# Graph network and expert feed-forward in one kernel: the feed-forward products go from fp32 to split 16-bit, with a software pipeline over groups of three tiles

## Chip, cores and metric

The kernel runs on one core of one Trainium2 chip. The metric is the device time of one execution in microseconds (us), as the median of several runs. The traces below come from one profiled execution.

## What is computed

`x` has 6250 rows of 256 features. A four-layer graph network is added to it; then a feed-forward part with two experts out of eight, chosen once for all rows, is added. Cut to what matters here:

```python
# graph part: 100,000 edges, 4 layers
h = layernorm(x) @ W_in + b_in
for l in range(4):
    msg = segment_sum((h * dinv)[src], dst) * dinv
    z = relu((h + msg) @ Wl[l] + bl[l] + mean(h) @ Wg[l] + bg[l])
    h = layernorm(z) * gamma[l] + beta[l]
x = x + h
# feed-forward part: the routing sees the mean over all rows, so both experts serve every row
xf = layernorm(x)
top_i, top_w = top2(softmax(scaled softmax(mean(xf) @ Wr + br)))
for e in top_i:                       # W1[e]: 256 x 512, W2[e]: 512 x 256
    h = gelu(xf @ W1[e] + b1[e]);  y += top_w[e] * (h @ W2[e] + b2[e])
x = x + layernorm(y + xf) * fgamma + fbeta
```

## The kernel before

The rows are cut into 49 tiles of 128 rows (`T`; the last, `LAST`, has 106). The kernel is written by hand, engine by engine: each engine has a program of its own, and semaphores (`wait_ge`) order them. No scheduler moves anything. Four stages follow each other.

First the adjacency counts are built and written to memory (to 548 us in the trace). Then come four graph layers, to 2806 us: for each of 49 tiles TensorE adds 49 products of 128x512 (`aggregate`, L1416), and inside this row of products it does the transposes and the six 16-bit products of the tile before (`turn_u` L1364 before product 14, `product_u` L1374 before product 24). VectorE has a chain of some fourteen instructions for each tile beside that (L923 to L840). GpSimd (Pool) does nothing there but, in the last layer, fetch `x` again (L604). Then the routing picks the two experts (`topi`), and SyncE loads their weights (L548, L553).

The feed-forward stage works on groups of three tiles (`SUP = RING = 3`, `LOOP = 16` groups and one more for tile 48). For a group TensorE does `up`: eight blocks `f` of hidden units, for each `KC = 2` products of 128 columns of `W1_s` with 384 rows of `xfT` in fp32. ScalarE applies Gelu from PSUM to SBUF (L1221, tile `gT`). Then come `turn` for the next group's three tiles (L1479, each copied from PSUM by ScalarE, L1216), and `down`: three tiles, each `TOP * FC = 8` fp32 products of 256 columns (L1496). An fp32 product is two MATMUL instructions in the trace. VectorE then normalizes each tile (`result`: L1027 adds the bias, L1031 and L1033 take mean and variance, Pool computes the inverse root, L610 and L612, and L1035 to L1044 finish). The loop over groups is a loop of the engines' programs, not written out.

The upward products wait for PSUM banks 0 to 2 in turn: block `f` waits for the Gelu of block `f - 3`. The downward products wait for all eight Gelus of their own group.

## Time and profile before

| | |
|---|---|
| median of 3 runs | 3208.35 us (3207.71 to 3212.56) |
| profiled execution, its own time | 3210.56 us |
| its span from the first to the last instruction | 3208.6 us |
| TensorE busy | 3076.7 us, 96% of the span |
| VectorE busy | 1901.3 us, 59% |
| ScalarE busy | 855.9 us, 27% |
| GpSimd (Pool) busy | 70.3 us, 2% |
| mean granted TensorE clock | 0.975 of full speed |
| by the chain that ended last | TensorE 84%, ScalarE 9%, VectorE 3% |

A row of the page or of a view gives line, engine, operation, the output and input tiles, shapes and a count; then busy time and the mean duration of one. A line number is a line of the kernel before. "PEld" is TensorE loading weights, which overlaps its products.

### The profile page before, as it was taken

The page shows a single profiled execution, that of the slowest core. Times are in us where ns is not written, and L with a number is a line of the kernel's source. Part 1 is how long each engine was busy: PE and PEld are TensorE (multiplying, and loading weights), DVE is VectorE, ACT ScalarE, POOL GpSimd, SP SyncE. Part 2 cuts the span into 40 slices and gives each one's busy share as a digit, 9 for nine tenths or more (in the row PEclk, how much of TensorE's full clock was granted, in tenths as well). Part 3 has the DMA queues.
Part 4 walks back from the last instruction along what each step waited for, and adds up shares of the span by engine and source line. Part 5 has one row for each costly group of instructions (what it writes and reads, how often), then busy time and mean ns, then how long its engine had stood idle before and what let it go on. Part 6 is the DMA issues. An engine that isn't in the chain of part 4 may idle for free.

```text
span 3208.6 us, 54202 instructions
## 1 busy us (share of the span) xinstructions
PE 3076.7 (96%) x17323; PEld 1804.0 (56%) x17323; DVE 1901.3 (59%) x5185; ACT 855.9 (27%) x1934; POOL 70.3 (2%) x168
## 2 busy tenths in 40 slices
PE   6999996999999999999999999999999999979998
PEld 4777773444444444444444444444444444468887
DVE  8999997555555545555554555555566666645554
ACT  4989896111111111111111111111111111132332
POOL 0000000000000000000000000000000000001010
PEclk9989996999999999999999999999999999989999
DMA  4323324122222222222222222222222222110000
GB/s 130 96 83 94 91 82 122 61 70 70 70 70 70 70 70 70 70 70 70 70 70 70 70 70 70 70 70 70 80 82 82 82 82 82 48 40 16 18 18 18
DMA packets 134110, 225.11 MB, mean 70 GB/s; under 512 B 12277, under 2 KB 106596, under 8 KB 134018
## 3 DMA queue, kind: packets, MB, share of 16 engines
q1 hardware_dynamic: 131666, 217.53, 20.9%
q0 software_dynamic: 2352, 6.40, 0.8%
q8 instruction: 52, 0.85, 0.1%
q14 instruction: 40, 0.33, 0.0%
HBM read 178.17 MB, written 45.74 MB: 70 GB/s over the span
## 4 chain that ended last, share of the span: by engine, by line
PE 84%; ACT 9%; DVE 3%; issue 2%; DMA 1%; SPq 0%; DVEq 0%; ACTq 0%; POOLq 0%; POOL 0%
PE bank L1416 64%; ACT tab L1094 7%; PE bank L1490 5%; PE bank L1496 5%; PE bank L1374 4%; PE bank L1364 1%; PE bank L1266 1%; PE bank L1286 1%; DVE later L757 1%; DMA tab<-in_x 1%; DVE region L724 1%; PE bank L1310 1%; ACT later L1118 0%; PE bank L1304 0%; ACT xnb L1112 0%
## 5 line engine op out<-in xcount | busy, mean ns | idle before, releaser
L1416 PE MATMUL bank<-tab,region 128*128 128x512 f16 x9604 | 2143.2, 380 | 14.3 <-DVE tab L840 14.0
L1416 PEld LDWEIGHTS bank<-tab,region 128*128 128x128 fp8e4 x9604 | 940.8, 98 | 1065.5 <-DVE tab L840 17.9
L1094 ACT ACTIVATE tab<-later 128x539 fp8e4<-128x539 uint8 x588 | 336.1, 674 | 1.9 <-DVE later L757 1.9
L724 DVE TENSOR_SCALAR region<-iota_w,src_col,src_w 128x540 bf16<-128x540 int16 x858 | 310.8, 415 | 0.4 <-issue 0.3
L941 DVE SCALAR_TENSOR_TENSOR region<-bank,c_back,later 128x256 f32<-128x256 f32 x196 | 94.8, 484 | 351.2 <-PE bank L1374 351.2
L1197 ACT ACTIVATE sd<-mv,eps_c 128x1 f32<-128x1 f32 x196 | 57.8, 295 | 817.6 <-DVE mv L948 817.6
L936 DVE TENSOR_TENSOR region<-bank,region 128x256 f16<-128x256 f32 x196 | 83.3, 425 | 287.7 <-ACT region L1193 287.7
L1193 ACT ACTIVATE region<-bank 128x256 f16<-128x256 f32 x196 | 75.3, 384 | 568.2 <-PE bank L1364 568.2
L1490 PE MATMUL bank<-tab 128*128 128x384 f32 (+1 forms) x544 | 178.0, 487 | 3.8 <-DMA b_s<-in_L_ffn_b 3.8
L1496 PE MATMUL bank<-tab 128*128 128x256 f32 (+1 forms) x784 | 175.5, 384 | 0.9 <-ACT tab L1221 0.9
L1490 PEld LDWEIGHTS bank<-tab 128*128 128x128 f32 x544 | 164.4, 310 | 13.4 <-issue 6.3
L1374 PE MATMUL bank<-later,region 128*128 128x256 f16 x1176 | 161.0, 273 | 0.9 <-DVE region L936 0.9
L1496 PEld LDWEIGHTS bank<-tab 128*128 128x128 f32 (+1 forms) x784 | 148.8, 192 | 22.3 <-ACT tab L1221 1.4
L1191 ACT ACTIVATE region<-bank 128x256 f32<-128x256 f32 x196 | 75.3, 384 | 294.0 <-PE bank L1416 294.0
L1161 ACT ACTIVATE tab<-region,c_write 128x256 f32 x147 | 74.6, 508 | 274.1 <-DVE region L957 274.1
L1374 PEld LDWEIGHTS bank<-later,region 128*128 128x128 f16 x1176 | 115.2, 98 | 56.3 <-DVE region L936 1.2
L1221 ACT ACTIVATE tab<-bank,b_s 128x384 f32<-128x384 f32 (+1 forms) x136 | 77.2, 568 | 249.3 <-PE bank L1490 249.3
L1286 PE MATMUL bank<-region 128*128 128x270 bf16 x900 | 131.0, 299 | 1.3 <-DVE region L708 0.8
L1286 PE MATMUL bank<-region,later 128*128 x864 | 129.3, 309 | 1.4 <-DVE region L724 1.4
L925 DVE TENSOR_TENSOR region<-bank,region 128x256 f32<-128x256 f32 x196 | 83.0, 423 | 73.9 <-ACT region L1191 73.9
L1286 PEld LDWEIGHTS bank<-region,later 128*128 128x128 f16 x864 | 112.7, 145 | 15.4 <-issue 2.5
L1286 PEld LDWEIGHTS bank<-region 128*128 128x128 f16 x900 | 108.7, 146 | 19.9 <-DVE region L724 1.8
(199 smaller groups left out, 2232.8 us busy)
## 6 DMA issues: line engine op xcount, KB each, us to landing
region<-adjacency SPq DMA_DIRECT2D x196, 784.0 KB, 4.3
adjacency<-tab SPq DMA_DIRECT2D x12, 3136.0 KB, 13.7
region<-in_x POOLq DMA_DIRECT2D x48, 128.0 KB, 2.3
out<-region SPq DMA_DIRECT2D x48, 128.0 KB, 1.7
tab<-in_x SPq DMA_DIRECT2D x1, 6016.0 KB
tab<-in_L_ffn_W SPq DMA_DIRECT2D x4, 512.0 KB, 4.7
region<-in_L_gnn_Wl SPq DMA_DIRECT2D x1, 1024.0 KB, 5.4
later<-in_L_gnn_Wg SPq DMA_DIRECT2D x1, 1024.0 KB, 9.4
```

The lines of the kernel that those rows point to most:

```text
L724: v.tensor_scalar(hot_s[:, j, :], iota_w[:, 0:WP], src_col[:, ds(first_block[0] + j, 1)], src_w[:, ds(first_block[0] + j, 1)], ALU.is_equa ...
L925: tile_own.done(v.tensor_tensor(acc_s, acc[a][:, 0:D], lo_f[:, a, :], ALU.add))
L936: v.tensor_tensor(uT[:, 1, :, :], T3[3], uT[:, 0, :, :], ALU.subtract).then_inc(uT_split, 1)
L941: tile_own.done(v.scalar_tensor_tensor(out=Z, in0=bank[4][:, 0:D], scalar=c_back[:, ds(n, 1)], in1=bias[:], op0=ALU.mult, op1=ALU.add))
L1094: ins = a.activation(stage[h][:, :, slot, f * LANES:f * LANES + n], counts[:, :, 0:n], ACT.Copy, saturate=False)
L1191: a.activation(lo_f[:, s, :], acc[s][:, D:2 * D], ACT.Copy).then_inc(lo_ready, 1)
L1221: a.activation(gT[:, f, 0:w], bank[f % 3][:, 0:w], ACT.Gelu, bias=b1_s[:, f // FC, f % FC:f % FC + 1]).then_inc(gelu_done, 1)
L1286: ins = mm(bank[k % 2 * 2 + half][:, 0:HALFP], hot_d[m % 2][:, :, j], hot_s[:, block + j, half * HALFP:(half + 1) * HALFP], start=j == 0, ...
L1374: ins = mm(bank[4][:, 0:D], uT[:, a, k, :], Wx[:, b, l, k, :], start=q == 0, stop=q == len(parts) - 1)
L1416: ins = mm(acc[a][:, :], A_s[:, a, m, :], tab[:, here + m, :], start=m == 0, stop=m == T - 1)
L1490: ins = mm(bank[f % 3][:, 0:w], W1_s[:, f // FC * KC + k, f % FC:FF:FC], xfT[:, k, 0:w], start=k == 0, stop=k == KC - 1)
L1496: ins = mm(bank[5 + u][0:r, 0:D], gT[:, f, u * P:u * P + r], W2_s[:, f // FC, f % FC, :], start=f == 0, stop=f == TOP * FC - 1)
```

## The change

The feed-forward products take 16-bit operands. Each fp32 operand is scaled and split into a high part (`fp16(scale * a)`) and a low part (what is left of it, also fp16), and three of the four products are added: high x high, high x low, low x high (`SPLIT`).

The weights are split once after they are loaded (ScalarE `w1_high_part`, `w2_high_part`; VectorE `w1_low`, `w2_low`). The transposed rows are split for each tile (ScalarE `xf_high`, VectorE `xf_low`), and the Gelu's output for each block (ScalarE `gelu`, two ACTIVATEs now, and VectorE `g_low`). The scales need bounds on the weights of all eight experts. They are made on Pool beside the first graph layer: it fetches `W1`, `W2` and `b1` of all experts in 32 pieces of 128x512 and one small one, squares each and adds it up. One 24-column product, one square root and some small VectorE instructions turn the sums into scales.

```diff
+            def fetch(c):
+                if c > 1:
+                    pool.wait_ge(scan_done, c - 1)
...
+                    nc.gpsimd.dma_start(scan_s[c % 2].rearrange("p (e c) -> p e c", e=EX),
+                                        pieces[c]).then_inc(scan_in[c % 2], 16)
...
+            for c in range(len(pieces)):
+                fetch(c + 1)
+                m = sums[c // each]
+                hold(pool, scan_in[c % 2], (c // 2 + 1) * 16)
+                square(scan_s[c % 2])
+                if c:
+                    pool.wait_ge(scan_done, c)
+                nc.gpsimd.tensor_tensor(m, m, scan_s[c % 2].rearrange("p (e c) -> p e c", e=EX),
+                                        ALU.add).then_inc(scan_done, 1)
```

The bias and the residual are added ahead of time on Pool, two additions of 128x256 for each tile; VectorE's part of a tile is five instructions instead of nine:

```diff
+            def residuals(t):
+                r = rows(t)
+                if t >= 3 * SUP:
+                    pool.wait_ge(y_taken, t - 3 * SUP + 1)
+                hold(pool, xf_ready, t + 1)
+                nc.gpsimd.tensor_tensor(xfb[0:r, t % (3 * SUP), :], xf_s[0:r, t % (2 * SUP), :], b2c[0:r, :],
+                                        ALU.add).then_inc(pre_done, 1)
+                nc.gpsimd.tensor_tensor(H[0:r, t, :], H[0:r, t, :], fbet[0:r, :], ALU.add).then_inc(pre_done, 1)
```

`gx`, the split Gelu output, has two buffers, and the loop is written out. TensorE now does all upward products of group `i`, then the transposes of group `i + 1`, then the downward products of group `i - 1`:

```diff
-                pe.wait_ge(gelu_done, (i + 1) * F8)
...
-                    pe.wait_ge(out_ready, (i + 1) * SUP)
-                    down(i * F8, u, P)
...
+            for i in range(GR + 1):
+                if i < GR:
+                    for f in range(TOP * FC):
+                        up(i, f)
+                for u in range(in_group(i + 1)):
+                    turn((i + 1) * SUP + u)
+                for u in range(in_group(i - 1)):
+                    down((i - 1) * SUP + u)
```

ScalarE's work for one block:

```diff
+            def gelu(i, f):
...
+                act.wait_ge(up_done, q + 1)
+                if q >= RING:
+                    act.wait_ge(g_split, q - RING + 1)
+                a.activation(gT[:, q % RING, 0:w], bank[q % RING][:, 0:w], ACT.Gelu, bias=b1_s[:, e, f % FC:f % FC + 1],
+                             scale=e_sel[:, e, 2:3]).then_inc(gelu_done, 1)
...
+                act.wait_ge(gelu_done, q + 1)
+                a.activation(gx[:, i % 2, 0, f, 0:w], gT[:, q % RING, 0:w], ACT.Copy,
+                             scale=g_scale[:, e:e + 1]).then_inc(g_high, 1)
```

TensorE, from the last upward block of a group to the next group, in the loop before (bank 3 and 4 hold transposes, banks 5 to 7 a tile's result):

```order
L1490 MATMUL bank1<-tab 128x384 [waits gelu_done]
L1490 MATMUL bank1<-tab 128x384
...
L1479 MATMUL bank3<-ident,region 128x128 [waits xf_ready]
...
L1479 MATMUL bank4<-ident,region 128x128 [waits xf_ready]
...
L1479 MATMUL bank3<-ident,region 128x128 [waits xfT_copied,xf_ready]
...
L1496 MATMUL bank5<-tab 128x256 [waits out_ready,ew_ready,gelu_done]
L1496 MATMUL bank5<-tab 128x256 x7
L1496 MATMUL bank6<-tab 128x256 [waits out_ready]
```

And the same place now, in the second turn of the loop:

```order
L1708 MATMUL bank0<-tab 128x384 [waits gelu_done]
L1708 MATMUL bank0<-tab 128x384 x5
L1693 MATMUL bank3<-ident,tab 128x128 [waits xfT_split,xf_ready]
...
L1693 MATMUL bank4<-ident,tab 128x128 [waits xfT_split,xf_ready]
...
L1693 MATMUL bank3<-ident,tab 128x128 [waits xfT_split,xf_ready]
L1693 MATMUL bank3<-ident,tab 128x128
L1723 MATMUL bank5<-tab,region 128x256 [waits w2_split,g_split]
L1723 MATMUL bank5<-tab,region 128x256 x23
L1723 MATMUL bank6<-tab,region 128x256 [waits w2_split,g_split]
```

A block is six 16-bit products for two fp32 ones, and a tile's downward row 24 for eight. The third transpose, which uses bank 3 again, waited for ScalarE's copy of the first; now it waits for VectorE's low part of the first (`xfT_split`).

VectorE, one turn of the loop now (L1191 is `g_low`, L1147 `xf_low`, L1142 `xf`, L1199 to L1215 the end of a tile of the group before):

```order
L1191 SCALAR_TENSOR_TENSOR region<-region,g_scale 128x384 [waits g_high] x8
L1147 SCALAR_TENSOR_TENSOR tab<-bank3,tab 128x2x128 [waits xfT_copied]
L1142 TENSOR_SCALAR tab<-tab,mv_all,rstd_all 128x256 [waits pre_done,xfT_done]
L1147 SCALAR_TENSOR_TENSOR tab<-bank4,tab 128x2x128 [waits xfT_copied]
...
L1199 SCALAR_TENSOR_TENSOR region<-bank5,y_scale,layer_rows 128x256 [waits pre_done,down_done]
L1202 BN_STATS st<-region 128x6 [waits y_taken]
L1204 BN_AGGR mv<-st 128x2 [waits dve_route]
L1209 SCALAR_TENSOR_TENSOR region<-region,mv,fgam 128x256 [waits fvar_ready]
L1215 SCALAR_TENSOR_TENSOR region<-region,rs,tab 128x256 [waits pre_done,out_out0,frstd_ready,dve_route]
```

Before, one tile's part was this, and nothing of the Gelus stood in VectorE's row:

```order
L1024 TENSOR_SCALAR region<-tab,mv_all,rstd_all 128x256
L1027 TENSOR_TENSOR region<-bank,tab 128x256 [waits down_done]
...
L1029 TENSOR_TENSOR region<-region 128x256 [waits dve_ffn]
...
L1031 BN_STATS st<-region 128x6 [waits dve_ffn]
...
L1033 BN_AGGR mv<-st 128x2 [waits dve_ffn]
L1035 TENSOR_SCALAR region<-region,mv,rs 128x256 [waits frstd_ready]
...
L1037 TENSOR_TENSOR region<-region,fgam 128x256 [waits dve_ffn]
...
L1039 TENSOR_TENSOR region<-region,fbet 128x256 [waits dve_ffn]
```

So the eight low parts and the first `xf_low` stand ahead of the tiles of the group before, and the third transpose, with all downward products behind it on TensorE, waits for them.

## Rows read from the trace of the kernel before

**Rows 1.** Window of the feed-forward loop: PE, PEld, DVE, ACT, POOL busy; PE clock.

```profile
2828.40:3185.60 357.20, 347.82 (x1373) 312.46 (x1374) 181.18 (x469) 107.88 (x189) 34.15 (x92) 0.99 0.06 19
```

**Rows 2.** Timeline of one group: start, us, engine, line (last: the next group).

```profile
3008.47 10.50 PE L1490 MATMUL bank<-tab 128*128 128x384 f32 x32
...
3009.98 0.58 ACT L1221 ACTIVATE tab<-bank,b_s 128x384 f32<-128x384 f32 x1 [10.03 <-PE bank L1490]
...
3020.25 10.59 PE L1496 MATMUL bank<-tab 128*128 128x256 f32 x48
...
3030.68 9.53 PE L1490 MATMUL bank<-tab 128*128 128x384 f32 x29
```

**Rows 3.** Timeline of the last layer: 16-bit products by their start times.

```profile
2782.72 2.32 PE L1416 MATMUL bank<-tab,region 128*128 128x512 f16 x10
...
2784.88 0.82 PE L1374 MATMUL bank<-later,region 128*128 128x256 f16 x6
...
2785.53 8.58 PE L1416 MATMUL bank<-tab,region 128*128 128x512 f16 x39
```

**Rows 4.** Groups by line, feed-forward stage: Gelu; busy, mean ns of one, idle.

```profile
L1221 ACT ACTIVATE tab<-bank,b_s 128x384 f32<-128x384 f32 x128 | 74.4, 582 | 233.9 <-PE bank L1490 233.9
...
L1221 ACT ACTIVATE tab<-bank,b_s 128x106 f32<-128x106 f32 x8 | 2.8, 350 | 15.5 <-PE bank L1490 15.5
```

**Rows 5.** Groups by line, first 548 us: ScalarE with two per-partition operands.

```profile
L1112 ACT ACTIVATE xnb<-tab,xnb_bias,xrs 128x256 f32<-128x256 f32 x49 | 28.9, 590 | 3.4 <-DVE xnb_bias L747 3.4
```

**Rows 6.** The page's costliest groups.

```profile
L941 DVE SCALAR_TENSOR_TENSOR region<-bank,c_back,later 128x256 f32<-128x256 f32 x196 | 94.8, 484 | 351.2 <-PE bank L1374 351.2
...
L1161 ACT ACTIVATE tab<-region,c_write 128x256 f32 x147 | 74.6, 508 | 274.1 <-DVE region L957 274.1
...
L1286 PEld LDWEIGHTS bank<-region,later 128*128 128x128 f16 x864 | 112.7, 145 | 15.4 <-issue 2.5
```

**Rows 7.** Timeline: VectorE behind a tile's downward products.

```profile
3001.77 0.42 DVE L1027 TENSOR_TENSOR region<-bank,tab 128x256 f32<-128x256 f32 x1 [4.59 <-PE bank L1496]
...
3004.56 0.41 DVE L1035 TENSOR_SCALAR region<-region,mv,rs 128x256 f32<-128x256 f32 x1 [1.09 <-POOL rs L612]
```

**Rows 8.** Windows, columns as in Rows 1: the granted clock around gaps.

```profile
290.30:293.70 3.40, 2.41 (x56) 2.02 (x56) 3.40 (x12) 3.06 (x9) 0.00 (x0) 1.00 0.02 5
293.80:297.10 3.30, 3.30 (x17) 2.46 (x16) 3.30 (x13) 2.69 (x6) 0.00 (x0) 0.50 0.00 0
...
2802.00:2806.00 4.00, 1.02 (x6) 0.29 (x5) 2.38 (x7) 1.06 (x3) 0.00 (x0) 0.99 0.00 0
2806.00:2828.00 22.00, 5.05 (x22) 3.22 (x22) 10.45 (x42) 4.37 (x13) 0.00 (x0) 0.50 0.23 65
...
2840.00:2843.50 3.50, 2.90 (x15) 2.34 (x14) 0.00 (x0) 2.28 (x6) 0.00 (x0) 1.00 0.00 0
```

**Rows 9.** Timeline: the first group's upward products.

```profile
2828.43 12.97 PE L1490 MATMUL bank<-tab 128*128 128x384 f32 x32 [3.79 <-DMA b_s<-in_L_ffn_b]
```

**Rows 10.** Timeline of a first-layer tile: VectorE's chain and TensorE.

```profile
700.73 0.49 DVE L929 SCALAR_TENSOR_TENSOR region<-region,c_own 128x256 f32<-128x256 f32 x1
...
702.09 0.38 PE L1364 MATMUL bank<-ident,region 128*128 128x128 f32 x2
...
710.04 0.49 DVE L840 SCALAR_TENSOR_TENSOR tab<-region,c_write,tab 128x256 f32 x1 [0.49 <-ACT tab L1161]
...
711.14 0.42 DVE L925 TENSOR_TENSOR region<-bank,region 128x256 f32<-128x256 f32 x1
```

**Rows 11.** Groups by line: Pool.

```profile
L595 POOL IOTA rep<- 128x2304 f16 x1 | 4.3, 4276 | 0.0
...
L573 POOL MEMSET tab<- 128x256 f32 x1 | 0.3, 312 | 0.2 <-POOL tab L569 0.2
```

**Rows 12.** Timeline: the last, 106-row group, and the last VectorE instruction.

```profile
3185.53 7.59 PE L1490 MATMUL bank<-tab 128*128 128x106 f32 x32
...
3203.86 0.42 DVE L1044 TENSOR_TENSOR region<-region,tab 106x256 f32<-106x256 f32 x1
```

More of the change, by code:

```diff
@@ L73 @@
 SUP = RING
+GR = LOOP + 1
+ZSCALE = 1024.0
+TINY = 1e-15
+SCAN = 512
 TURN_AT, PRODUCT_AT = 0, 8
@@ new lines, in square, with total @@
+            def square(x):
+                own.done(nc.gpsimd.tensor_tensor(x, x, x, ALU.mult))
+                own.hold()
+            def total(sums, width, to):
+                while width > 1:
+                    width //= 2
+                    own.hold()
+                    own.done(nc.gpsimd.tensor_tensor(to if width == 1 else sums[:, :, 0:width], sums[:, :, 0:width],
+                                                     sums[:, :, width:2 * width], ALU.add))
+            sums = [w[:, 0:SCAN].rearrange("p (e c) -> p e c", e=EX) for w in (src_col, src_w)]
@@ new lines, in _ @@
+            for m in sums:
+                own.done(nc.gpsimd.memset(m, 0.0))
+            own.wait()
+            fetch(0)
+            for c in range(len(pieces)):
[7 more added lines that the diff above has]
+                                        ALU.add).then_inc(scan_done, 1)
@@ L601, in again @@
+            hold(pool, scan_done, len(pieces))
+            hold(pool, scan_in[0], (len(pieces) // 2 + 1) * 16)
+            for k, m in enumerate(sums):
+                total(m, width, e_lim[:, k * EX:(k + 1) * EX].unsqueeze(2))
+            square(scan_s[0][:, 0:EX * FC])
+            total(scan_s[0][:, 0:EX * FC].rearrange("p (e c) -> p e c", c=FC), FC, e_lim[:, 2 * EX:].unsqueeze(2))
+            own.wait()
+            pool.sem_inc(lim_set, 1)
             def again(t, i, u, r):
@@ L1058, in _ @@
-            route_own.wait()
-            dve.sem_inc(ew_ready, 1)
-            with dve.Fori(0, LOOP - 1) as i:
+                xf(SUP + u)
+            w1_low(1)
+            dve.wait_ge(b2_in, 16 * TOP)
+            own.done(v.tensor_scalar(b2c[:], b2_s[:, 0, :], topw[:, 0:1], None, ALU.mult))
+            own.wait()
+            v.scalar_tensor_tensor(out=b2c[:], in0=b2_s[:, 1, :], scalar=topw[:, 1:2], in1=b2c[:],
+                                   op0=ALU.mult, op1=ALU.add).then_inc(ew_ready, 1)
@@ new lines, in ffn, with mine, before, after @@
+            def ffn(i):
+                def mine(f):
+                    if i < GR:
+                        g_low(i, f)
+                def before(u, step):
+                    if u < in_group(i - 1):
+                        step((i - 1) * SUP + u)
+                def after(u):
+                    if u < in_group(i + 1):
+                        xf_low((i + 1) * SUP + u)
+                    if u < in_group(i + 2):
+                        xf((i + 2) * SUP + u)
+                for f in range(TOP * FC):
+                    mine(f)
@@ L1073, in _ @@
+                    before(u, result)
+                if i == 0:
+                    for a in range(TOP):
+                        w2_low(a)
+            for i in range(GR + 1):
+                ffn(i)
         @block.scalar
@@ L1457, in _ @@
                 general()
+            pe.wait_ge(lim_set, 1)
+            mm(bank[6][:, 0:3 * EX], ones[:], e_lim[:], start=True, stop=True).then_inc(lim_sum, 1)
             pe.wait_ge(hsum_ready, LAYERS + 1)
```

314 lines of the change are left out of this document (214 added, 100 removed).

## The prediction, made before the changed kernel ran

> **What bounds the kernel now.** I read the busy times by stage first. The change touches two places: the feed-forward stage from 2828.43 us on, and Pool in the first layer. In the feed-forward loop TensorE is busy 347.8 of 357.2 us [rows 1], so it is the bound there, and the chain of waits says the same. The timeline of one group shows how: 32 upward instructions in about 10.5 us, transposes, 48 downward ones in about 10.6, and the next group 22.2 us after the last (3030.68 - 3008.47) [rows 2]. ScalarE has one Gelu of 0.58 us for every 1.29 us of upward work and waits for TensorE in between; it is far from a bound. Two readings of the same trace then decide what replaces this: what the new ScalarE and VectorE work costs, and what TensorE's clock does after a gap.
>
> **TensorE's work.** 16-bit products stream at a pace that depends on their columns: ten of 512 columns start in 2.16 us (2784.88 - 2782.72), 0.216 each; six of 256 in 0.65 us (2785.53 - 2784.88), 0.108 each [rows 3]. A product of 384 columns is halfway, 0.162. An upward block of six is 0.97 us, a group's eight blocks 7.8 us. Three tiles of 24 downward products are 72 x 0.108 = 7.8 us. The weights of the upward products are read with a step of four elements. A strided 16-bit weight load took 145 ns with a step of 18 elements [rows 6], still under 162, so I cost it at nothing; if it passed 162 it would add 48 times the excess to a group. Alone TensorE would need about 16 us for a group against 22.2, and the loop would win some 95 us. It will not be alone.
>
> **ScalarE's work.** For each block it now has a Gelu with two per-partition operands and a copy from SBUF with one. Two operands took 590 ns and one 508 for 256 columns [rows 5, 6], so the second costs 0.08 and the Gelu becomes 0.582 + 0.08 = 0.66. The slope is (582 - 350) / (384 - 106) = 0.83 ns a column [rows 4], so the copy, 508 ns at 256, becomes 0.61 at 384. The copy waits for the Gelu's own end (I take 0.04 for the hand-over), and the next Gelu may start about 0.1 before the copy ends. That is 1.22 us for a block. It is longer than the 0.97 that TensorE takes, but TensorE may be three blocks ahead, so its upward row still ends after 7.8 us; ScalarE ends after 0.97 + 0.22 (from a block's last product to its Gelu: 3009.98 - 3008.47 - 1.29 [rows 2]) + 8 x 1.22 + 0.1 = 11.1 us.
>
> **Where the stall goes.** The order of the instructions puts the third transpose behind `xfT_split` of the first tile. ScalarE's copies of the transposes stand behind its eighth block, and VectorE's `xf_low` behind its eighth `g_low`. A VectorE instruction of this kind took 484 ns at 256 columns [rows 6]; at 384 I take 0.62 (between 0.48 and 0.73, one and a half times it). So: 11.1 + 0.65 (`g_low`) + 0.5 (`xf_low`) + 0.3 (third transpose and the first weights) = 12.5, and 12.5 + 7.8 = 20.3 us for a group, at full clock. TensorE does nothing but four small transposes between 7.8 and 12.2 us. This stall is in each of the 16 full groups but for the last, which has a small group behind it. What comes late next are the downward products.
>
> **The clock.** A gap like this is in the trace. Between 2802 and 2806 us TensorE was busy 1.0 of 4.0 us, and the granted clock is 0.50 (1.2 GHz) afterwards; in 290.3 to 293.7, with 2.4 us of busy time that was mostly 49 one-column products, it fell too, and the next 3.3 us have 0.50. In the loop of before, 2840 to 2843.5, TensorE was busy 2.9 of 3.5 us and the clock stayed at 1.00 (2.4 GHz) [rows 8]. The new gap, some 0.7 us of work in 4.5, looks like the two that fell. What a low clock costs: the first group's 32 upward instructions, begun at it, took 12.97 us where the same row took 10.50 [rows 2, 9], 2.5 us. If the low stretch is as short as the one in rows 8 (3.3 us) and lies wholly over downward products, it costs half of that, 1.65. I take 1.8 (bounds 0 and 2.5), and the group becomes 22.1 us, almost what it was.
> The Trainium skill (TensorE: Matmul & The Clock Gate, section HAM oscillation) says the same of loops: a wait in every turn that puts the engine idle for several microseconds brings the half clock back in every turn, and its cost is paid each time. It speaks against this change; without that rule the group would be 20.3.
>
> **VectorE behind the products.** From L1027 to the end of Pool's answer took 2.79 us (3004.56 - 3001.77) [rows 7]. One addition goes (0.46), the fused one is 0.06 longer, and one of 0.48 follows: 2.9 us for a tile, while its products take 2.6. So VectorE ends a group 12.5 + 2.6 + 3 x 2.9 = 23.8 us after its start, 3.5 us into the next at full clock, and then does `g_low` of block 0 (to 4.1). ScalarE needs that for its fourth Gelu, at 1.2 + 3 x 1.22 = 4.9. The cover is 0.8 us; a tile of over 3.2 us uses it up.
>
> **The loop's sum.** The first group has no downward row: at the low clock its first block takes 1.95, so 1.95 + 0.22 + 9.9 + 0.65 + 0.5 + 0.3 = 13.5. Fifteen groups at 22.1 are 331.5. Then come the 106-row group (48 products bound by weight loads of about 0.1 us, 4.8), 7.8 and 2.6 of downward products, a wait for VectorE's tiles (about 3), a last tile of 2.9, and about 1 of low clock: 22. Together 367.0 us. Before, from 2828.43 to the end of the last VectorE instruction (3204.28) it was 375.9 [rows 9, 12]. The loop gives 9 us.
>
> **Setup.** The weight loads are issued at the same point. Behind their landing stand now two splits of an expert's first half on ScalarE (0.7 each) and VectorE (0.75); but the first expert's matrix no longer waits for the second's. Bounds -0.5 and +2; I take +0.3. The new root and scale instructions lie beside the routing sum, which waits for TensorE anyway.
>
> **Pool in the first layer.** 32 pieces, each a fetch, a square and an addition of 128x512, and four rows of halving sums. The trace has no such instruction. The nearest are a memset of 256 columns in 0.31 us and an iota at 1.86 ns a column (4276 / 2304) [rows 11]; so 0.6 to 1.9 us each, and I take 1.0, 64 us of work spread over 150 to 200 us of transfers. Nobody waits for it. It costs only if it slows VectorE, of which the trace shows nothing: no arithmetic of Pool on 128 columns or more runs beside VectorE's there. In this layer VectorE has little to spare. U is ready at 701.22 and TensorE's transpose starts at 702.09, 0.9 us; the chain's end at 710.53 is 0.6 before the next tile's L925 at 711.14 [rows 10]. Bounds: 0, and 30 us if each of 64 instructions holds VectorE for half its length and no slack takes it. Against some 15 tiles with 0.9 us of slack each, I take 6 us.
>
> **Sum.** 3210.56 (this execution's own time; the median is 2.2 lower) - 9 + 0.3 + 6 = 3207.9; against the median, 3205.7. I write 3206: no change that a measurement of this kernel can tell, which is about 0.2%, 6.4 us. Its own range is 3194 to 3216.
>
> **Rivals.**
> *The clock holds.* The two new gaps in rows 8 that fell had less work than 0.7 us in 4.5, or one-column work; the new one has four transposes, and if ScalarE's pair is 1.15 instead of 1.22 the gap is 0.6 shorter. Then 13.5 + 15 x 20.3 + 21 = 339 us, 37 less than before: 3208.35 - 37 + 6.3 = 3178. Chance 0.17.
> *Pool's scan holds VectorE.* Place: the first layer, from 548 us. Pool's squares and additions and VectorE's instructions take turns at the memory; each holds the other up. VectorE's chain has at most 0.9 us to give to a tile, so it decides once the delays pass that: nine of its instructions read two tensors or one at double pace, and three delays of 0.5 us in a tile are 1.5, 0.6 over. At half of 1.0 us for 64 instructions, 30 us: 3208.35 - 9 + 30 = 3229. For it: VectorE's small slack. Against it: transfers of 256-byte pieces leave Pool waiting most of the time. Chance 0.2.
> The Trainium skill (SBUF — State Buffer, section Who interferes with whom) states such a lock between a GpSimd instruction that reads and a VectorE instruction with two SBUF inputs; no run here shows it yet.
> *VectorE's tiles become the bound.* Pool now has two additions a tile (0.5 to 1.0 us each by rows 11) beside its 0.75 us for the root. If they delay VectorE's last instruction so that a tile takes 3.9 us instead of 2.9, `g_low` of block 0 ends at 7.1 instead of 4.1, 2.2 past ScalarE's need: a group of 23.5 or so with some low clock, 15 x 1.4 more: 3227. It decides from 3.2 us on. Chance 0.12.
> *The split is cheaper than I think* (a copy of 0.5, say): 8 x 0.11 less a group, 14 us: 3192. Chance 0.06.
> The forecast keeps 0.45.
>
> **How the numbers follow.** The forecast lies around 3206 with about half of it between 3202 and 3215, a third of it below. Faster by over 0.2% (under 3202): 0.17 + 0.06 + 0.45 x 0.35 = 0.39. Slower (over 3215): 0.2 x 0.75 + 0.12 + 0.45 x 0.1 = 0.31. Same: 0.30. The range leaves out a piece of the first two rivals at either side: 3176 to 3230.
>
> **What would show it.** Right: upward rows of 48 in 7.8 us; a gap of about 4 us ahead of each third transpose, released by VectorE's L1147; windows of 0.50 clock in the downward rows; groups 22 us apart; ScalarE pairs of 1.22; in the first layer steps of 11.5 to 12.5 us while Pool scans. Wrong: groups at 20 us with the clock at 1.00 throughout; layer steps of 13 us; a first-layer stage more than 15 us longer; L1191 of block 0 as the releaser of the fourth Gelu. An upward row that stretches beyond 7.8 us (strided weights) would make it wrong too.

## The result and the profile after

The changed kernel takes 3261.3 us (median of 4, 3256.0 to 3265.6) against 3208.0 (3207.5 to 3212.6): the ratio is 1.0165, interval 1.0153 to 1.0177. It is 53 us slower, and 31 us above the upper end of my range.

By stages (the windows of the kernel after; each row has the stretch, its length, the busy time of PE, its weight loads, DVE, ACT and POOL, then the granted clock):

```profile
548.00:1106.00 558.00, 522.09 (x2537) 253.88 (x2538) 305.63 (x686) 72.05 (x183) 112.35 (x115) 0.97 0.25 81
1106.00:2806.00 1700.00, 1698.30 (x8448) 835.07 (x8447) 910.41 (x2444) 218.11 (x593) 24.18 (x45) 1.00 0.22 73
...
2860.00:3200.00 340.00, 262.50 (x1746) 192.99 (x1746) 210.51 (x417) 159.80 (x285) 115.21 (x174) 0.92 0.07 22
```

Two stages have holes in TensorE's time. In the first layer (548 to 1106) it is idle for 36 of 558 us, and Pool, which had almost nothing to do there, is busy for 112. In the feed-forward loop it is idle for 77 of 340 us, and the clock is 0.92 in the mean. The loss is counted from the starts of TensorE's rows. The first tile's product in the first layer began at 567.08 before and begins at 573.02 now; the last tile's began at 2805.96 and now begins at 2842.06:

```profile
573.02 0.82 PE L1583 MATMUL bank<-later,region 128*128 128x256 f16 x6
590.59 0.82 PE L1583 MATMUL bank<-later,region 128*128 128x256 f16 x6
```
```profile
2842.06 0.98 PE L1583 MATMUL bank<-later,region 128*128 128x256 f16 x6 [0.94 <-DVE region L1045]
2864.61 10.55 PE L1708 MATMUL bank<-tab 128*128 128x384 f16 x48 [3.63 <-DVE tab L1180]
2880.80 9.32 PE L1708 MATMUL bank<-tab 128*128 128x384 f16 x48 [1.17 <-DVE tab L1147]
```

So the layers are 36.1 us longer: 5.9 ahead of the first product, and 30 in the next six steps, which take 17.6, 14.9, 15.6, 19.6, 14.3 and 16.6 us where each took 11.45 (578.53 less 567.08, say). The seventh takes 11.65, and behind it the steps are as before. From there to the first upward product it is 22.6 us, as before (22.5 to the row of [rows 9]). The loop, to the end of VectorE's last instruction, takes 391.1 us instead of 375.9 [rows 9, 12]: 15.2 more. Together that is 51.4, the difference of the two spans.

**The first layer.** VectorE's groups of instructions from 575 to 640 us, while Pool scans the weights (busy us, mean ns, then the idle time before them):

```profile
L1063 DVE TENSOR_TENSOR region<-region,layer_rows 128x256 f32<-128x256 f32 x4 | 6.9, 1719 | 0.3 <-DVE region L1061 0.2
L954 DVE SCALAR_TENSOR_TENSOR later<-region,valid,later 128x256 f32<-128x256 f32 x4 | 6.1, 1524 | 0.4
L1061 DVE TENSOR_SCALAR region<-region,mv,rs 128x256 f32<-128x256 f32 x4 | 3.6, 910 | 0.1
L1055 DVE BATCH_NORM_STATS2 st<-region 128x6 f32<-128x256 f32 x4 | 1.7, 428 | 0.4
L1045 DVE TENSOR_TENSOR region<-bank,region 128x256 f16<-128x256 f32 x4 | 1.7, 425 | 4.4 <-ACT region L1375 4.4
```
and Pool's in the whole scan (the 16 squares of the other buffer, the row of `dstf`, waited 3.1 us for their transfers):
```profile
L660 POOL TENSOR_TENSOR srcf<-srcf 128x512 f32<-128x512 f32 x16 | 16.8, 1049 | 2.9 <-DMA srcf<-in_L_ffn_W 2.6
L653 POOL DMA_DIRECT2D dstf<-in_L_ffn_W x16 | 15.0, 936 | 4.8 <-POOL src_col L681 2.1 <-POOL src_w L681 2.1 <-POOL src_w L671 0.3
L681 POOL TENSOR_TENSOR src_col<-src_col,dstf 128x512 f32<-128x512 f32 x8 | 10.4, 1301 | 1.1
```

The multiplication by gamma (L1063) reads two tensors of SBUF: 1719 ns. L1061 reads one: 910, and it took 412 without the scan (s0_no_scan below). The two that stay at their length, 425 and 428 ns, read one operand from PSUM (L1045), or take statistics of one tensor (L1055). Pool's own instructions hardly wait for VectorE: all 32 squares take 1.03 to 1.05 us and 30 of the 32 additions 1.26 to 1.27; only two take 1.53. And Pool waited for data for only 2.6 and 3.1 us in front of its 32 squares.

**The loop.** One group on the timeline (start, duration, and in brackets the wait and its releaser):

```profile
3037.01 0.53 PE L1693 MATMUL bank<-ident,tab 128*128 128x128 f32 x2 [3.98 <-DVE tab L1147]
3037.33 9.62 PE L1723 MATMUL bank<-tab,region 128*128 128x256 f16 x72
3041.74 0.48 DVE L1199 SCALAR_TENSOR_TENSOR region<-bank,y_scale,layer_rows 128x256 f32<-128x256 f32 x1 [3.01 <-PE bank L1723]
3043.20 0.41 POOL L702 TENSOR_SCALAR sd<-mv 128x1 f32<-128x1 f32 x1 [14.29 <-DVE mv L1204]
3043.76 0.55 POOL L704 TENSOR_TENSOR rs<-sd,half_c 128x1 f32<-128x1 f32 x1
3044.28 0.73 POOL L711 TENSOR_TENSOR layer_rows<-tab 128x256 f32<-128x256 f32 x1
3044.40 0.89 DVE L1215 SCALAR_TENSOR_TENSOR region<-region,rs,tab 128x256 f32<-128x256 f32 x1 [0.83 <-POOL rs L704]
3044.96 0.91 POOL L713 TENSOR_TENSOR tab<-tab,fbet 128x256 f32<-128x256 f32 x1
3045.21 0.47 DVE L1199 SCALAR_TENSOR_TENSOR region<-bank,y_scale,layer_rows 128x256 f32<-128x256 f32 x1
3046.78 6.01 PE L1708 MATMUL bank<-tab 128*128 128x384 f16 x36
3052.11 2.13 DVE L1191 SCALAR_TENSOR_TENSOR region<-region,g_scale 128x384 f16<-128x384 f32 x3
3053.29 0.67 ACT L1421 ACTIVATE region<-bank,b_s,e_sel 128x384 f32<-128x384 f32 x1 [1.39 <-DVE region L1191]
3054.01 2.44 PE L1708 MATMUL bank<-tab 128*128 128x384 f16 x12 [1.22 <-ACT region L1421]
3060.87 0.50 PE L1693 MATMUL bank<-ident,tab 128*128 128x128 f32 x2 [3.98 <-DVE tab L1147]
```
and two windows, the start of its downward row and the whole group behind it (columns as before; the granted clock is the number behind POOL's):
```profile
3037.30:3040.60 3.30, 3.30 (x18) 2.35 (x16) 1.28 (x4) 0.38 (x1) 0.00 (x0) 0.50 0.00 0
3046.80:3070.60 23.80, 18.50 (x128) 13.73 (x126) 14.37 (x30) 10.55 (x19) 7.49 (x13) 0.93 0.06 17
```

The gap ahead of the third transpose is where I put it, 3.98 us. The 72 downward products behind it take 9.62 us, the first 3.3 of them at a clock of 0.50. VectorE's three tiles start 3.45 us apart (3041.74, 3045.21, 3048.66); its last instruction of a tile, L1215, takes 0.89 us beside Pool's L711 and L713. So the first `g_low` comes at 3052.11, and it takes 1.08 us itself, beside the third tile's L713 on Pool, where it is 0.61 in the kernel without the additions. The fourth Gelu waits 1.39 for it, and TensorE, at most three blocks ahead, waits 1.22. The group takes 23.86 us; it was 22.2 [rows 2].

### The profile page after: what moved, and what is told of

It reads as the page before. It is cut to its first block, busy times and chain, and to the rows that moved or that the text cites. A ratio compares the mean times of both kernels' runs of the same rounds, so it can differ in the third digit from the quotient of the medians.

```text
span 3260.0 us, 55441 instructions
## 1 busy us (share of the span) xinstructions
PE 3025.1 (93%) x17989; PEld 1705.5 (52%) x17989; DVE 1994.0 (61%) x5193; ACT 924.9 (28%) x2064; POOL 271.9 (8%) x380
## 4 chain that ended last, share of the span: by engine, by line
PE 73%; ACT 11%; DVE 7%; issue 5%; POOL 1%; DMA 1%; DVEq 1%; SPq 0%; ACTq 0%; POOLq 0%
PE bank L1625 61%; ACT tab L1276 7%; PE bank L1583 4%; PE bank L1723 2%; ACT region L1421 2%; PE bank L1573 1%; PE bank L1475 1%; PE bank L1495 1%; POOL rs L704 1%; DVE later L866 1%; DMA tab<-in_x 1%; DVE region L1199 1%; DVE st L1202 1%; POOL sd L702 1%; PE bank L1519 1%
## 5 line engine op out<-in xcount | busy, mean ns | idle before, releaser
L1625 PEld LDWEIGHTS bank<-tab,region 128*128 128x128 fp8e4 x9604 | 942.3, 98 | 1069.7 <-DVE tab L949 17.6
L1045 DVE TENSOR_TENSOR region<-bank,region 128x256 f16<-128x256 f32 x196 | 83.3, 425 | 281.7 <-ACT region L1375 281.7
L695 POOL DMA_DIRECT2D region<-in_x x49 | 26.4, 540 | 2107.6 <-DVE tab L1075 2106.2
L1708 PE MATMUL bank<-tab 128*128 128x384 f16 (+1 forms) x816 | 140.5, 327 | 26.0 <-ACT region L1421 19.7
L1723 PE MATMUL bank<-tab,region 128*128 128x256 f16 (+1 forms) x1176 | 154.5, 301 | 0.0
L1723 PEld LDWEIGHTS bank<-tab,region 128*128 128x128 f16 (+1 forms) x1176 | 127.9, 109 | 24.6
L1421 ACT ACTIVATE region<-bank,b_s,e_sel 128x384 f32<-128x384 f32 (+1 forms) x136 | 87.7, 645 | 168.3 <-PE bank L1708 147.4
L1708 PEld LDWEIGHTS bank<-tab 128*128 128x128 f16 x816 | 88.3, 115 | 74.4 <-ACT region L1421 32.2
```

The lines of the kernel that those rows point to most:

```text
L1045: v.tensor_tensor(uT[:, 1, :, :], T3[3], uT[:, 0, :, :], ALU.subtract).then_inc(uT_split, 1)
L1421: a.activation(gT[:, q % RING, 0:w], bank[q % RING][:, 0:w], ACT.Gelu, bias=b1_s[:, e, f % FC:f % FC + 1], scale=e_sel[:, e, 2:3]).then_in ...
L1625: ins = mm(acc[a][:, :], A_s[:, a, m, :], tab[:, here + m, :], start=m == 0, stop=m == T - 1)
L1708: ins = mm(bank[q % RING][:, 0:w], W1x[:, b, f // FC * KC + k, f % FC:FF:FC], xfT[:, i % 2, c, k, 0:w], start=n == 0, stop=n == 3 * KC - 1)
L1723: ins = mm(bank[5 + u][0:r, 0:D], gx[:, i % 2, b, f, u * P:u * P + r], W2x[:, c, f // FC, f % FC, :], start=n == 0, stop=n == 3 * TOP * FC ...
```

## The experiments

Two losses, each with a candidate: Pool's scan in the first layer, and Pool's additions in the loop. Behind them stands the third question, whether the gap and the clock cost what I said. The names that begin with s concern the scan, those with g the loop, those with c both.

**s0_no_scan**: the scan is replaced by constants.

```diff
-            for c in range(len(pieces)):
-                fetch(c + 1)
...
-                square(scan_s[c % 2])
...
+            own.done(nc.gpsimd.memset(e_lim[:, 0:EX], 4.0))
```

> The whole scan is left out: the bounds of the weights are three constants, so scales and output differ. In the trace of the changed kernel the first layer's products begin 5.9 us later than before and their first seven steps take 30.1 us more than 11.45 each. Theory A (the scan costs all of that): first product back at 567 us, all steps 11.45, layers 36 us shorter, 3261 - 36 = 3225. Theory B (the start of the layers is later for another reason, as the moved rows of layer weights or the longer program): the steps come back but not the 5.9 before them: 3231. Rival: the loss was in neither, and the time stays above 3250.

3227.5 us (3224.9 to 3228.9), ratio to before 1.0062 [1.0045, 1.0079]: 33.8 less than the changed kernel. The first product begins at 564.7 and all steps are 11.45:

```profile
564.68 0.82 PE L1567 MATMUL bank<-later,region 128*128 128x256 f16 x6
```

L1063's counterpart is back at its length (VectorE's groups of this kernel, 575 to 640 us):

```profile
L938 DVE SCALAR_TENSOR_TENSOR later<-region,valid,later 128x256 f32<-128x256 f32 x6 | 2.9, 484 | 0.8
L1047 DVE TENSOR_TENSOR region<-region,layer_rows 128x256 f32<-128x256 f32 x6 | 2.6, 426 | 0.2
L1045 DVE TENSOR_SCALAR region<-region,mv,rs 128x256 f32<-128x256 f32 x6 | 2.5, 412 | 0.2
```

The whole loss of the layers, the 5.9 us at their start among it, is the scan's: without its arithmetic the first product begins at 563.4 to 566.5 us in the traces (six kernels), with the whole of it at 570.5 to 573.4 (five). That start moves by some 3 us from trace to trace.

**s1_fetch_only** and **s2_arith_only**: its two halves.

```diff
 s1_fetch_only
                 hold(pool, scan_in[c % 2], (c // 2 + 1) * 16)
-                square(scan_s[c % 2])
...
+                pool.sem_inc(scan_done, 1)
 s2_arith_only
-                fetch(c + 1)
-                hold(pool, scan_in[c % 2], (c // 2 + 1) * 16)
                 square(scan_s[c % 2])
```

> The 32 transfers stay, with their waits; squares, additions and sums on Pool are left out, the bounds are constants (output differs). Theory A (Pool's arithmetic holds VectorE): within 3 us of the kernel without any scan, about 3226, VectorE's additions of two tensors back at 0.42 us. Theory T (the transfers, of 256-byte pieces, or their issue on Pool of 0.92 us each, hold VectorE or the adjacency's transfers): still 20 us or more above it, 3245 to 3260.

> The reverse: 32 squares and 32 additions of 128x512 on Pool back to back on zeros, no transfers, constants as bounds (output differs). Without fetches of 0.92 us in between the 64 instructions take 64 x 1.15 = 74 us instead of 123. Theory A: the loss is one for each Pool instruction that overlaps VectorE's, so it is about as large as before, 25 to 40 us, but in fewer tiles, 4 or 5 instead of 7; 3250 to 3262. Theory T: no loss, 3226.

3227.3 and 3253.4 us (one run each). The 32 transfers with their issue on Pool cost the kernel nothing that shows, though they stretch some of VectorE's instructions a little (one with one SBUF operand, L1051, is 452 ns instead of 412). The arithmetic alone brings 26 of the 34 us back, in three steps of 17.7, 17.3 and 17.3 us and a first product 10 us later. The 8 us that neither half shows by itself come only with both, where the same arithmetic is spread over 126 us instead of 75; what makes them was not tested. Rows of s2_arith_only (VectorE's from 592 to 627 us, then Pool's):

```profile
L1063 DVE TENSOR_TENSOR region<-region,layer_rows 128x256 f32<-128x256 f32 x2 | 2.7, 1372 | 0.1
```
```profile
L660 POOL TENSOR_TENSOR srcf<-srcf 128x512 f32<-128x512 f32 x16 | 18.0, 1126 | 0.0
```

**s5_one_input**: the same transfers, but each Pool instruction reads one operand.

```diff
-                square(scan_s[c % 2])
+                own.done(nc.gpsimd.tensor_scalar(scan_s[c % 2], scan_s[c % 2], 1.0, None, ALU.mult))
...
-                nc.gpsimd.tensor_tensor(m, m, scan_s[c % 2]..., ALU.add).then_inc(scan_done, 1)
+                nc.gpsimd.tensor_scalar(scan_s[c % 2], scan_s[c % 2], 1.0, None, ALU.mult).then_inc(scan_done, 1)
```

> The scan's transfers and waits as in the changed kernel, but each of its 64 Pool instructions of two operands is one of a single operand on the same 128x512 (a product with 1.0); the sums are left out and the bounds are constants. Theory A1 (it is Pool's two reads that hold VectorE): first layer within 5 us of the kernel without a scan: 3228 to 3232. Theory A2 (any Pool instruction that reads SBUF does, by its length): the loss falls only with the length of the instructions, from 1.05 to 1.27 us to perhaps 0.8: 20 to 25 us stay, 3247 to 3252.

3232.6 us (one run): 5 above the kernel without a scan, 29 below the changed one, although Pool's instructions became longer, not shorter (Pool in the scan, then VectorE from 575 to 640 us):

```profile
L678 POOL TENSOR_SCALAR srcf<-srcf 128x512 f32<-128x512 f32 x16 | 24.1, 1507 | 1.0 <-DMA srcf<-in_L_ffn_W 0.5
```
```profile
L1062 DVE TENSOR_TENSOR region<-region,layer_rows 128x256 f32<-128x256 f32 x5 | 3.6, 723 | 0.2
L953 DVE SCALAR_TENSOR_TENSOR later<-region,valid,later 128x256 f32<-128x256 f32 x5 | 2.6, 530 | 0.6
L1060 DVE TENSOR_SCALAR region<-region,mv,rs 128x256 f32<-128x256 f32 x5 | 2.7, 548 | 0.2
```

Theory A2 falls: 97 us of Pool's one-operand work cost 5 us, 75 of its two-operand work (32 squares, 32 additions) cost 34. VectorE's instructions in the rows are still stretched, by 0.05 to 0.3 us instead of 0.5 to 1.3, and most of that goes into the slack of a tile. The edit changes the number of operands and with it the kind of instruction, and no run parts the two.

**g0_no_adds**: the two additions out of the loop.

```diff
-                nc.gpsimd.tensor_tensor(xfb[...], xf_s[...], b2c[0:r, :], ALU.add).then_inc(pre_done, 1)
-                nc.gpsimd.tensor_tensor(H[0:r, t, :], H[0:r, t, :], fbet[0:r, :], ALU.add).then_inc(pre_done, 1)
+                pool.sem_inc(pre_done, 1)
+                pool.sem_inc(pre_done, 1)
```

> Only the feed-forward loop changes: Pool's two additions a tile (expert bias into the normalised rows, beta into the residual) are left out, so the output lacks both and the first reads stale rows. Scan as in the changed kernel. Theory A (they lengthen VectorE's tile from 3.05 to 3.45 us, which delays g_low of the first block and with it the fourth Gelu by 1.39 us): tile 3.05, the fourth Gelu's wait 0.2, its block's stall on TensorE gone, groups 22.6 instead of 23.86, 16 x 1.26 = 20 us less: 3241. Rival: the tile is set by Pool's own root pair (0.41 + 0.55) and stays at 3.4: 3258. Rival: the wait goes but TensorE's gap grows by the same, since ScalarE's eight pairs set it: groups 23.6, 3257.

3240.9 us (3238.1 to 3247.2), ratio 1.0106 [1.0089, 1.0123]: 20.4 less. L1215's counterpart takes its 485 ns again (VectorE's groups of this kernel), tiles are 3.06 us apart, and groups 22.02 and 22.36 in turn behind the first two, 22.2 on the mean; `g_low` of block 0 is back at 0.61 us:

```profile
L1214 DVE SCALAR_TENSOR_TENSOR region<-region,rs,tab 128x256 f32<-128x256 f32 x21 | 10.2, 485 | 17.6 <-POOL rs L704 17.6
```

**g3_filled**: more work in the gap (`FILL` is 30), with the output unchanged.

```diff
+                    if u == 2 and i:
+                        pe.wait_ge(y_taken, (i - 1) * SUP)
+                        for n in range(FILL):
+                            mm(bank[5][:, 0:D], gx[:, i % 2, 0, 0, 0:P], W2x[:, 0, 0, 0, :], ...)
                     turn((i + 1) * SUP + u)
```

> More work and nothing else: in the gap ahead of the third transpose TensorE does 30 products of 256 columns into a bank that is overwritten behind them (3.25 us); the output is unchanged. Theory A (the gap lowers the clock, which costs the downward row 1.7 us a group): clock 1.00 in the loop, 72 downward products in 7.8 instead of 9.6 us; VectorE's tiles then begin 0.9 earlier and the next upward row 1.7 earlier, so the fourth Gelu waits some 0.3 longer; groups 22.4 to 22.6, 15 x 1.3 = 20 us less: 3241. Rival (the downward row is slow from weights or reads, not the clock): groups 23.9, 3261. Rival (the filling delays the transpose): over 3261.

3237.9 us (3236.1 to 3240.5), ratio 1.0092 [1.0075, 1.0109]: 420 more products made the kernel 23.5 us faster. TensorE's rows of this kernel, and one group's window:

```profile
3066.73 3.44 PE L1739 MATMUL bank<-tab,region 128*128 128x256 f16 x30
3070.88 0.41 PE L1694 MATMUL bank<-ident,tab 128*128 128x128 f32 x2 [0.71 <-DVE tab L1148]
3071.13 8.02 PE L1724 MATMUL bank<-tab,region 128*128 128x256 f16 x72
```
```profile
3056.80:3079.00 22.20, 20.16 (x159) 15.88 (x157) 14.41 (x30) 10.55 (x19) 7.56 (x13) 1.00 0.06 20
```

The transpose comes at the same distance from its group's start, released by the same instruction; only the clock differs, 1.00 instead of 0.93, and the downward row takes 8.02 instead of 9.62 us. The group, 22.20 us, is 1.66 shorter: that is the price of the clock, 1.8 in my sum.

**g1_turn_late**: the gap's other cure, by order.

```diff
-                for u in range(in_group(i + 1)):
+                for u in range(min(2, in_group(i + 1))):
                     turn((i + 1) * SUP + u)
-                for u in range(in_group(i - 1)):
+                for u in range(min(2, in_group(i - 1))):
                     down((i - 1) * SUP + u)
+                if in_group(i + 1) > 2:
+                    turn((i + 1) * SUP + 2)
+                if in_group(i - 1) > 2:
+                    down((i - 1) * SUP + 2)
```

> Full computation; only TensorE's order changes: of each group's three transposes the third goes behind two of the three downward tiles, so the 4 us in which TensorE waited for xf_low of the first tile hold 48 downward products. VectorE's order stays: xf_low of the third tile, which now comes late, stands ahead of all three tiles' normalisation. Theory A (a group is upward row, gap and downward row in line, with the clock's fall on top): no gap over 2 us, clock 1.00 in the loop, and VectorE in line becomes the bound: its three tiles (10.4 us) can begin only at about 15 us and end at 25.4, ScalarE's fourth Gelu waits for them, then five more pairs: groups 21 to 22, about 23.86 - 2.2, 15 x 2.2 = 33 us less: 3228, 3220 to 3240. Rival (the gap only moves, to the third transpose's copy): 23 to 24, 3250 to 3262.

3260.0 us (3258.2 to 3261.1), ratio 1.016 [1.0143, 1.0177]: nothing gained, groups 23.9 us. My 3228 was wrong. The downward row is whole, but the gap stands in the upward row now (ScalarE's and TensorE's rows of this kernel, and one group's window):

```profile
3051.40 2.13 DVE L1191 SCALAR_TENSOR_TENSOR region<-region,g_scale 128x384 f16<-128x384 f32 x3
3052.57 0.67 ACT L1421 ACTIVATE region<-bank,b_s,e_sel 128x384 f32<-128x384 f32 x1 [5.08 <-DVE region L1191]
3053.30 4.03 PE L1708 MATMUL bank<-tab 128*128 128x384 f16 x12 [4.91 <-ACT region L1421]
```
```profile
3042.30:3066.20 23.90, 18.99 (x129) 13.98 (x127) 14.32 (x30) 10.55 (x19) 7.57 (x12) 0.86 0.05 17
```

That VectorE's order becomes the bound I had said, at 21 to 22 us; that the new gap lowers the clock again, for longer (0.86 in the group), I had not put into the sum. Behind it twelve products take 4.03 us at a clock of 0.50; at the pace of 36 in 6.01 us (the changed kernel at 3046.78) it would be 2.0.

**g2_tiles_between**: VectorE's order too.

```diff
+                before(i - 2, 1, gathered)
+                before(i - 2, 1, centred)
+                normal_of(1)
+                before(i - 2, 1, result)
...
-                for f in range(TOP * FC):
+                for f in range(1, TOP * FC):
                     mine(f)
...
+                before(i - 1, 0, gathered)
```

> Full computation; TensorE's order as in g1_turn_late, and VectorE's normalisation of the second and third tile of a group stands between the first g_low of the next group, the wait for Pool's root of each tile filled with other work. Theory A (the loss in the loop is order, not work): TensorE has 7.8 + 0.9 + 7.8 = 16.5 us of work for a group at full clock, VectorE about 16, and the groups come 16.5 to 18 us apart with the clock at 1.00; 15 x 6.6 = 99 us less: 3162 (3150 to 3185). Rival (Pool's and VectorE's instructions stretch each other, so VectorE's 16 become 18.5 or more): 19 us, 3190. Rival (ScalarE's chain through the copies of the transposes is the bound): over 20 us, 3205 or more.

3180.0 us (3176.4 to 3182.7), ratio 0.9914 [0.9897, 0.993]: 81 less than the changed kernel, with all of its work, and faster than the kernel before. The gain expected was 99, with groups of 16.5 to 18 us; they are 18.13. VectorE's instructions are still stretched here (L1218, the last of a tile, 906 ns). The clock is 1.00 through the group and the holes are 1.4 of 18.1 us (one group's window of this kernel):

```profile
3039.00:3057.10 18.10, 16.67 (x128) 12.99 (x127) 14.33 (x30) 10.66 (x19) 7.62 (x13) 1.00 0.07 24
```

**s4_scan_on_act**: the scan's arithmetic on ScalarE, in the last layer.

```diff
+                    if last and s < 2:
+                        act.wait_ge(scan_in[s], 16 * (i + 1))
+                        a.activation(scan_s[s], scan_s[s], ACT.Square,
+                                     accum_out=part_sq[:, s, ds(i, 1)]).then_inc(scan_done, 1)
```

> Full computation; the squares and sums of the expert weights go from Pool in the first layer to ScalarE in the last: one piece of 128x512 (2 KB in a row per partition) in two of three tiles, one Square with a running sum each, about 0.7 us, put where ScalarE waits over 4 us for VectorE. Pool keeps only the fetches and the 32 columns of the bias. Theory A (only Pool's arithmetic beside VectorE's costs): first layer as without a scan, last layer 0 to 3 us longer: 3227 to 3230. Rival (ScalarE's extra instruction delays the copies on the tile's chain): 0.7 in 32 tiles, 3250. Rival (the function's table is loaded anew each time, 1.28 us twice per tile): 3290 or more.

3227.3 us (3226.1 to 3228.8), ratio 1.006 [1.0043, 1.0077]: as without a scan. Its 32 squares lie in ScalarE's waits (ScalarE's groups of this kernel, 2260 to 2800 us):

```profile
L1361 ACT ACTIVATE dstf<-dstf 128x512 f32<-128x512 f32 x16 | 9.9, 622 | 0.0
```

**c1_both**, **c2_order**, **c3_early**: all of it together, then two steps more. The edit of c2 to VectorE's order, and that of c3 to Pool's:

```diff
 c2_order
                 before(i - 2, 1, result)
+                mine(0)
                 before(i - 2, 2, gathered)
                 before(i - 2, 2, centred)
                 normal_of(2)
-                mine(0)
+                mine(1)
                 before(i - 2, 2, result)
-                for f in range(1, TOP * FC):
+                for f in range(2, TOP * FC):
 c3_early
             for i in range(GR + 1):
+                for u in range(in_group(i)):
+                    beta(i * SUP + u)
                 for u in range(SUP):
...
-                nc.gpsimd.tensor_tensor(H[0:r, t, :], H[0:r, t, :], fbet[0:r, :], ALU.add).then_inc(pre_done, 1)
```

> Full computation: g2_tiles_between and s4_scan_on_act together. If the two losses are independent the gains add: the one was 3261.3 - 3180.0 = 81.3 us below the changed kernel, the other 34.0: 3146 (3143 to 3150), about 2% faster than the kernel before. Rival (they share something, as the clock or the start of the feed-forward): over 3155.

> c1_both with VectorE's first two g_low of a group one place earlier: the first ahead of the third tile's normalisation, the second ahead of its last instruction. In g2_tiles_between the fourth Gelu waited 0.9 us and the fifth 0.5 for these two (groups 18.13 us). Theory A (VectorE's order still sets the group): waits of 0 and 0.3 remain, groups 17.2, 15 x 0.9 = 13 us less than c1_both: 3133. Rival (VectorE's amount of work sets it, 18 us a group however ordered): equal to c1_both within 3 us.

> c2_order with one of Pool's two additions a tile (beta into the residual, 0.91 us) moved from behind each tile's root to where Pool waited 8.4 us a group for the first tile. Theory A (VectorE's last instruction of a tile is stretched from 0.48 to 0.89 by both additions, one after the other): at least 0.15 us less a tile if one of them is enough for part of the stretch, 0.4 if the second one did it, so 0 to 1.2 us a group where VectorE is the bound: 3118 to 3133, I take 3127. Rival (the addition now stretches g_low, 0.62 us, which is as critical): 3133 or a little more.

Medians of 5 with the ratio to the kernel before: c1_both 3146.8, 0.9805 [0.9792, 0.9818]; c2_order 3139.1, 0.9786 [0.9772, 0.9799]; c3_early 3134.3, 0.977 [0.9756, 0.9783]. The two cures add to within a microsecond of the 3146 expected. The two later steps gave 8 and 5 us where I said 13 and 6; the groups of the three are 18.14, 17.78 and 17.3 us. In c3_early VectorE's last instruction is still long, 917 ns as in c2_order, so the one addition that was left behind the root is enough to stretch it; and `g_low` is longer, 782 ns instead of 737, eight times a group, which may be why c3 gained little (VectorE's groups, 2930 to 3060 us, then a window of one group):

```profile
L1180 DVE SCALAR_TENSOR_TENSOR region<-region,g_scale 128x384 f16<-128x384 f32 x58 | 43.8, 782 | 6.5 <-ACT region L1436 6.5
L1207 DVE SCALAR_TENSOR_TENSOR region<-region,rs,tab 128x256 f32<-128x256 f32 x24 | 22.0, 917 | 5.2 <-issue 5.2
```
```profile
2983.36:3000.66 17.30, 16.51 (x129) 13.08 (x127) 15.00 (x30) 10.66 (x19) 7.87 (x13) 1.00 0.07 24
```

TensorE is now busy 16.5 of 17.3 us, so about 0.8 us a group is all that order can still give. This is the gain that the 16-bit products were able to have: 22.2 to 17.3 us a group, 74 us in all.

## Why the prediction was wrong

The forecast was 3206: loop -9, setup +0.3, scan +6. Measured by the traces: loop +15.2, setup +0.1, layers +36.1.

**The scan: the rival held, and my term was mis-sized.** I took 6 us from bounds of 0 and 30, and it is 36.1 in the traces, 33.8 by s0_no_scan. The place and the wait were the rival's: VectorE's instructions stand still beside Pool's, and its chain decides the tile. The rival's "each holds the other up" is hardly true of Pool: of its 64 instructions two took 0.27 us longer. (Without fetches in between, in s2_arith_only, its squares were held somewhat: 1.03 to 1.48 us.) The rival's bound came out too, as 64 instructions at half of their mean length of 1.16 us are 64 x 0.58 = 37 us, but the half was a guess, and VectorE's single instruction lost far more than half of one of Pool's. What failed is the step "64 us of work spread over 150 to 200 us of transfers", by which 15 tiles with 0.9 us of slack each would take most of it. Pool hardly waited for its transfers (5.7 us in front of its squares and 2.2 in front of its issues) and went through the 32 pieces from 547.8 to 674.1 us, 3.9 us each, 3.3 of them busy. So the meetings were dense, and six steps took 30 us, 5 each, against a slack of 0.9; what little slack there is was used some seven times, not fifteen. The instruction took 1.05 to 1.3 us where I had 1.0. The trace before could not show the lock. It did show a transfer of 128 KB on the same queue that lands 2.3 us after its issue; the 256 KB of a piece land in 3.7 to 3.9, no more than Pool needs for the issue, square and addition of the piece before (its turn of 3.9). The time of a piece could not be known from the trace before, but the short landing could. The cause of the bad weight was "against it: transfers of 256-byte pieces leave Pool waiting most of the time".
The Trainium skill (SBUF — State Buffer, section Who interferes with whom) states that a VectorE instruction with two SBUF inputs contends with a GpSimd instruction that reads SBUF. The rows agree: 1719 ns for 426, while instructions with one operand in PSUM keep 425. They also show what that sentence leaves open: Pool's squares and additions cost 34 us, its one-operand instructions 5 (s5_one_input). I gave that rule 0.2; by the prediction's own count of instructions it would have given 3229 and, with 37 instead of 30, 3236.

**VectorE's tile: the second rival held as well.** I had 2.9 us for a tile with a limit of 3.2, and it is 3.45: 3.06 without Pool's additions, 0.4 for them (g0_no_adds). Pool's first instruction behind L1204 is the likely source of the other 0.16: L702 takes 0.41 us beside VectorE's L1209, where its counterpart L610 took 0.19 with VectorE waiting. The limit agrees with the runs: at 3.06 the fourth Gelu no longer waits, at 3.45 it waits 1.39. But I had priced the rival at a tile of 3.9 to give a group of 23.5, and 3.45 already gave 23.86, 1.66 more than the 22.2 without the additions. Three tiles of 0.39 more are 1.17 of that, and the stretch of the first `g_low`, 1.08 us for 0.61, is the rest; I had no term for it. That ScalarE's pair is 1.27 us (I had 1.22) doesn't explain it, since g0_no_adds has the same pairs. In the sum fourteen groups take 23.8 us on average (2880.80 to 3214.10) instead of 22.1, 24 us more. The fifteenth takes only 16.3, because the last full group has no stall; I had said so and yet put it into the sum at 22.1, which gives 5.8 back.

**The clock, the gap and the products: right.** The gap is 3.98 us (some 4), released by L1147; the fall costs 1.66 us a group (1.8) and 36 upward products take 6.01 us (5.8). The rival that the clock holds, 0.17, is refuted by the 0.50 in the downward row and by g3_filled. Its argument had misread a row: the gap of 2802 to 2806 us held 1.02 us of work in 4.00, more than the 0.7 in 4.5 of the new one, not less, so the rows spoke against this rival more strongly than I let them. With g0_no_adds the group is 22.2, for the 22.1 of my sum.

**The two ends of the loop.** The first group took 16.2 us, I had 13.5: I let the low clock last for one block, but it lasted 5.3 us into the upward row (48 products in 10.55 us; the clock from 2864.6 to 2869.9 us is 0.50, then 1.00), and where no downward row stands behind the third transpose, the next upward row waits for its copies too (1.17 us), which I had not counted. The tail took 25.3, I had 22: the small group's upward row waits for VectorE's tiles (3.25 us), which I had counted only behind the downward products.

Taken one by one out of the changed kernel, the two interferences are 33.8 and 20.4 us; less both it would be 3207.1, next to the forecast of 3206. Part of that nearness is luck: the forecast holds 6 us for the scan, which the 3207.1 doesn't, and without them it would be 7 too low. Most of the 7 is in the loop, which takes 371.9 us in g0_no_adds where I had 367.0. The sum was not run as one kernel; c1_both shows that cures of the two places add.

Both rivals look like one mechanism, an instruction of Pool that reads beside one of VectorE that reads: the stretch goes when Pool's instructions go, in either place. That Pool's one-operand work costs far less was tested only in the scan. I had treated the two as independent with 0.20 and 0.12. One price wrong made both come in, and the range, which allowed for either alone, did not hold the two.

## What to carry to other kernels

Work given to an idle engine is free only if it leaves the memory alone that a chain needs. Before Pool gets additions beside VectorE's, count VectorE's instructions with two operands in SBUF on that chain and take up to a full Pool instruction as the price of a meeting (0.4 us in the loop, 1.3 in the scan). Compare that with the slack of one turn of the chain. How many turns pay depends on how fast Pool gets through its work, so compare the landing of a transfer with Pool's own time for a piece. ScalarE did the same sums in its waits at no cost that shows.

A faster product makes the order of the other engines the bound. Here 23.9 us became 17.3 without taking out any work, and moving only TensorE's order gave nothing: the gap went from the downward row into the upward row and took the clock's fall with it.

Rivals that rest on the same untested lock should share one chance, and the range should hold the sum of both.

## What the runs showed of the hardware that I had not expected

- Pool's one-operand instruction on 128x512 took 1.51 us, longer than its square (1.05) or addition (1.27 to 1.30) of two operands; and it held VectorE far less: 5 us in all against 34.
- Some of VectorE's one-operand instructions are held too: L1061 took 910 ns instead of 412, while the statistics of one tensor kept their 428.
- In the scan the hold went almost one way. The instructions of VectorE that it reached lost 0.5 to 1.3 us each on the mean; Pool's 32 squares kept 1.03 to 1.05 us.
- The stretch in the scan is about a whole Pool instruction: L1063 went from 426 to 1719 ns, +1.29, where Pool's take 1.05 to 1.30.
- 30 added products in a gap made each group 1.66 us shorter, by the granted clock alone.
- Pool's issue of 32 transfers, 0.9 us each, cost the kernel nothing measurable (3227.3, one run, against 3227.5 us), though L1051 took 452 ns beside them instead of 412.
